# A transformer block on one core: one burst of value products a head, four side slots, and halves and sums made on other engines

## What is computed

```
mod = (silu(c) @ wmod).reshape(4, 6, 1, 512);  sa, ca, ga, sb, cb, gb = mod[:, 0..5]
ga, gb = sign * maximum(abs, 0.25)
h = layernorm(x) * (1 + ca) + sa
q = (h @ q_w.T + q_b) as 16 heads of 32;  k = h @ k_w.T + k_b;  v = h @ v_w.T + v_b
scores = q @ k.T / sqrt(32), future keys masked
x = x + ga * (softmax(scores) @ v, heads joined, @ o_w.T + o_b)
h = layernorm(x) * (1 + cb) + sb
h = fwht(h * SU_ug) / 64
h = silu(h @ W_gate.T * s_gate) * (h @ W_up.T * s_up)
x = x + gb * (fwht(h * SU_dp) / 64 @ W_down.T * s_dp)
```

## Time and profile before

| | us |
|---|---|
| median of three runs | 1978.73 |
| lowest and highest | 1975.44, 1981.24 |
| the profiled execution, its own time | 1982.4 |
| its span | 1980.6 |
| attention, heads 0 to 63, within it | about 57 to 904 |
| TensorE busy | 1902.7 |
| VectorE busy | 1392.6 |
| ScalarE busy | 833.0 |
| GpSimd busy | 462.1 |

### The profile page before, as it was taken

The page is one execution under the profiler, slowest core; times in us unless marked ns, Lnnn a source line. Parts: engine busy times, 40 slices in busy tenths (PEclk is TensorE's granted clock), DMA queues, the critical chain, the costliest instruction groups (busy, mean ns, idle before and its releaser), DMA issues.

```text
span 1980.6 us, 39650 instructions
## 1 busy us (share of the span) xinstructions
PE 1902.7 (96%) x15040; PEld 1582.5 (80%) x15040; DVE 1392.6 (70%) x3247; ACT 833.0 (42%) x1551; POOL 462.1 (23%) x525
## 2 busy tenths in 40 slices
PE   6999999999999999999999999999999999999998
PEld 3677777777777667667888789999999999999997
DVE  6788787777668666684467797777676777767755
ACT  3366455555555554473222442333333323333221
POOL 2244455445444444362010010010000100101000
PEclk8899999999999999999999999999999999999999
DMA  7432243333332455635347989778788797887884
GB/s 228 131 97 67 77 122 102 94 82 96 107 109 60 130 167 172 221 123 177 138 138 281 359 312 347 286 288 333 287 314 323 294 345 287 291 329 290 330 306 165
DMA packets 118709, 416.19 MB, mean 210 GB/s; under 512 B 26349, under 2 KB 39917, under 8 KB 104313
## 3 DMA queue, kind: packets, MB, share of 16 engines
q1 hardware_dynamic: 106856, 363.27, 53.7%
q10 hardware_dynamic: 11664, 50.40, 6.7%
HBM read 318.16 MB, written 61.10 MB: 191 GB/s over the span
## 4 chain that ended last, share of the span: by engine, by line
PE 46%; DVE 5%; ACT 2%; DMA 1%; issue 1%; SPq 0%; POOL 0%; DVEq 0%; ACTq 0%
PE banks L1810 22%; PE banks L1900 15%; PE banks L1680 8%; PE banks L1776 1%; DVE ln_stats L1254 1%; PE banks L1770 1%; DMA upgate_items_dram<-items_ring 1%; DVE x_normed L1266 0%; DVE y L1379 0%; DMA upgate_raw<-in_w_ug 0%; ACT silu_gate L911 0%; ACT y_split L896 0%; ACT L911 0%; ACT L917 0%; DVE out_sb L1451 0%
## 5 line engine op out<-in xcount | busy, mean ns | idle before, releaser
L1900 PE MATMUL banks<-d_ring,y_split 128*128 128x512 f32 x1536 | 377.6, 393 | 1.9 <-DVE y_split L1399 1.9
L1007 ACT ACTIVATE probs<-banks 128x512 f32<-128x512 f32 x576 | 314.8, 600 | 149.6 <-PE banks L1946 145.7
L1900 PEld LDWEIGHTS banks<-d_ring,y_split 128*128 128x128 f32 x1536 | 281.9, 188 | 56.6 <-DVE y_split L1399 2.1
L1810 PE MATMUL banks<-h_t_split,items_ring 128*128 128x256 f32 x2280 | 321.2, 284 | 1.9 <-DVE both L1356 1.9
L1810 PEld LDWEIGHTS banks<-h_t_split,items_ring 128*128 128x128 f32 x2280 | 299.0, 191 | 13.7 <-ACT h_t L822 4.0
L1734 PE MATMUL banks<-k_stack,q_stacks 96*128 96x512 f32 (+3 forms) x768 | 255.5, 376 | 26.7 <-DVE max_all L1166 12.4
L1946 PE MATMUL banks<-q_stacks,k_stack 98*128 98x512 f32 (+3 forms) x768 | 254.2, 373 | 4.5 <-DMA q_stacks<-neg_max_rows 3.9
L1810 PE MATMUL banks<-input_sums,items_ring 128*128 128x256 f32 x1710 | 236.2, 283 | 0.0
L1108 POOL TENSOR_TENSOR probs<-probs 128x1024 f32<-128x1024 f32 x64 | 153.4, 2396 | 334.0 <-ACT probs L1007 334.0
L1978 PE MATMUL banks<-probs,values 128*32 128x128 f32 (+1 forms) x3328 | 222.8, 322 | 3.1 <-POOL probs L1128 3.1
L1810 PEld LDWEIGHTS banks<-input_sums,items_ring 128*128 128x128 f32 x1710 | 218.9, 192 | 0.0
(11 more groups left out here) (180 smaller groups left out, 2715.1 us busy)
## 6 DMA issues: line engine op xcount, KB each, us to landing
items_ring<-upgate_items_dram SPq DMA_DIRECT2D x94, 1792.0 KB, 7.3
d_ring<-down_split_dram SPq DMA_DIRECT2D x128, 512.0 KB, 8.1
q_stacks<-q_split SPq DMA_DIRECT2D x192, 128.0 KB, 2.9
upgate_raw<-in_w_ug SPq DMA_DIRECT2D x32, 512.0 KB, 4.8
upgate_items_dram<-items_ring ACTq DMA_DIRECT2D x8, 1792.0 KB, 7.5
upgate_items_dram<-items_made ACTq DMA_DIRECT2D x8, 1792.0 KB, 6.7
x<-in_x SPq DMA_DIRECT2D x32, 256.0 KB, 3.0
o_group<-o_and_sums SPq DMA_DIRECT2D x256, 32.0 KB
```

Of the source, the lines that this page charges most:

```text
L1007: nc.scalar.activation(pr[:, probs_slot(H, u), :], score_bank[:, at % SLOTS_SCORE, :], ACT.Exp, scale=SCALE).then_inc(exped, 1)
L1810: last = nc.tensor.matmul(item_bank(g, item), weights[:, a, item, k * P:(k + 1) * P], by_key(item_input(blk, item, m))[:, k, :], start=(k ...
L1900: last = nc.tensor.matmul(acc[:, t, :], ys[s][:, a, t * P:(t + 1) * P], dr[g % D_RING][:, m, :], start=(f == 0 and a + m == 0), stop=(f == ...
```

## The change

Four things are changed together.

- **The burst.** `weigh` runs both parts of head H - 1 one behind the other after unit 5 of head H. The table WEIGHED is laid out anew: part 0 has 14 instructions where it had 21, part 1 has 23 where it had 24. Part 1 still waits for GpSimd's sums and masks. GpSimd adds the probabilities of unit 7 too (`sum_last`, a third add of 512 columns behind the last masks of the head), so the products of unit 7's blocks with ones fall away. The transposition of the maxima moves from unit 2, where it stood ahead of the maxima product, to unit 5, behind it. ScalarE still copies it behind the exponential of unit 2, in the order of its own program.
- **The banks.** All heads share one output bank; the part 0 of a head waits until the head before has been evacuated. The bank that comes free is a fourth side slot.
- **High halves.** `modulate` and `keys_values` on ScalarE read the slot twice and write the rounded high half themselves, ahead of the unrounded copy; the two casts on VectorE are gone.
- **Folds.** The w_down tiles at unit 4 move to unit 5. Their two sets of loads share one set of semaphores.

The core of the diff:

```diff
 PART_ENDS, PARTS_OF_HEAD = (4, 8), 2
+WEIGH_UNIT, SCORES_AHEAD = 5, 3
 WEIGHED = [
-    [(0, 0, (0, 4)), (1, 0, (1, 5)), (2, 0, (2, 6)), (3, 0, (3, 7)), (0, "sum", ((0, 3), (6, 7))), (1, "sum", ((0, 2), (6, 6))),
+    [(0, 0, (0, 4)), (1, 0, (1, 5)), (2, 0, (2, 6)), (3, 0, (3, 7)), (0, "sum", ((0, 3), (6, 7))), (1, "sum", ((6, 6),)),
...
-    if 0 < H < heads - 1:
-        units[TOP_UNIT].append(("top", H + 1))
     if 0 < H < heads - AHEAD:
         for i in range(NS):
             units[i].append(("max", H + AHEAD, i))
+    if 0 < H < heads - 1:
+        units[WEIGH_UNIT].append(("top", H + 1))
...
-    SLOTS_SCORE, SLOTS_SIDE = 3, 3
-    score_bank, side, obank = banks[:, 0:3, :], banks[:, 3:6, :], banks[:, 6:8, :]
+    SLOTS_SCORE, SLOTS_SIDE = SCORES_AHEAD, 4
+    score_bank, side, obank = banks[:, 0:3, :], banks[:, 3:7, :], banks[:, 7, :]
...
-                nc.scalar.activation(kv[:, i % 2 * HALF:(i % 2 + 1) * HALF], side[:, r, :], ACT.Identity,
-                                     bias=mod[:, 0, k, b:b + 1], scale=mod[:, 1, k, b:b + 1]).then_inc(side_free[r], 1)
+                for out in (ht[:, 0, k, h * HALF:(h + 1) * HALF], kv[:, i % 2 * HALF:(i % 2 + 1) * HALF]):
+                    last = nc.scalar.activation(out, side[:, r, :], ACT.Identity, bias=mod[:, 0, k, b:b + 1], scale=mod[:, 1, k, b:b + 1])
+                last.then_inc(side_free[r], 1)
...
                     side_step(ends[u])
-                    if u == PART_ENDS[0] and H:
+                    if u == WEIGH_UNIT and H:
                         evacuate(H - 1)
-                    side_step(units[u])
+                    side_step([key for key in units[u] if key[0] != "top" or H == 0])
+                    if u == WEIGH_UNIT - SCORES_AHEAD and H:
+                        side_step([key for key in units[WEIGH_UNIT] if key[0] == "top"])
...
+            def sum_last(H):
+                pool.wait_ge(summed, 3 * H + 2)
+                pool.wait_ge(masked, H * len(TRIANGLES) + list(TRIANGLES).index(SUM_AFTER) + 1)
+                nc.gpsimd.tensor_tensor(pr[:, PR_SLOTS - 2, :], pr[:, PR_SLOTS - 2, :], pr[:, probs_slot(H, SUM_AFTER), :], ALU.add).then_inc(summed, 1)
...
-                chain.link(nc.vector.tensor_copy(ht[:, 0, k, at], kv[:, i % 2 * HALF:(i % 2 + 1) * HALF]))
...
-                chain.link(nc.vector.tensor_copy(kst[0:96, b % 2, at], kv[0:96, at]))
...
-                    if H >= 2:
-                        pe.wait_ge(o_copied, H - 1)
+                    if H:
+                        pe.wait_ge(o_copied, H)
...
-                    if u == PART_ENDS[0] and H:
-                        weigh(H - 1, 1)
-                    if u == (PART_ENDS[1] if H else FIRST_WEIGHED):
-                        weigh(H, 0)
-            weigh(ALL - 1, 1)
+                    if u == WEIGH_UNIT and H:
+                        for part in range(PARTS_OF_HEAD):
+                            weigh(H - 1, part)
+            for part in range(PARTS_OF_HEAD):
+                weigh(ALL - 1, part)
```

More of the change, by code:

```diff
@@ L52 @@
 WEIGHED = [
[L53 to L60 removed]
+    [(0, 0, (0, 4)), (1, 0, (1, 5)), (2, 0, (2, 6)), (3, 0, (3, 7)), (0, "sum", ((0, 3), (6, 7))), (1, "sum", ((6, 6),)),
+     (2, 1, (2, 6)), (3, 1, (3, 7)), (1, 1, (1, 5)), (0, 1, (4,)), (2, 2, (2, 6)), (3, 2, (3, 7)), (0, 2, (4,)), (1, 2, (5,))],
+    [(0, 3, (4,)), (1, 3, (5,)), (2, 6, (6,)), (3, 3, (3, 7)), (0, 4, (4,)), (1, "sum", ((0, 2),)), (2, 3, (6,)),
+     (0, "sum", ((1, 3), (5, 7))), (1, 4, (5,)), (2, 4, (6,)), (3, 6, (7,)), (1, 5, (5,)), (2, 5, (6,)), (3, 4, (7,)),
+     (0, "sum", ((3, 3), (7, 7))), (1, "sum", ((1, 2), (5, 6))), (2, "sum", ((0, 1), (5, 5))), (3, 5, (7,)), (3, 7, (7,)),
+     (0, "sum", ((2, 3), ("all", 7))), (1, "sum", ((2, 2), ("all", 6))), (2, "sum", ((1, 1), ("all", 5))),
+     (3, "sum", ((0, 0), ("all", 4)))],
 ]
@@ L92 @@
 PART_ROWS = 32
-PART_BANKS = (6, 7)
+PART_BANKS = (2, 7)
 BESIDE_MAXIMA = {("max", 0, 2 * k + 1): k for k in range(KT)}
@@ L100 @@
 PROJECTION_STEPS = (1, 5)
-FOLDS = [("across", left, u) for left, us in ((18, (4, 8)), (17, (4, 8)), (16, (4, 8)), (15, (2, 4, 6, 8)), (14, (4, 8)), (13, (4, 8)), (12, (4, 8))) for u in us]
-FOLDS += [("along", left, u) for left, us in ((10, (4, 8)), (9, (4, 8)), (8, (4, 8)), (7, (2, 4, 6, 8)), (6, (4, 8)), (5, (4, 8)), (4, (4, 8))) for u in us]
+FOLDS = [("across", left, u) for left, us in ((18, (5, 8)), (17, (5, 8)), (16, (5, 8)), (15, (2, 4, 6, 8)), (14, (5, 8)), (13, (5, 8)), (12, (5, 8))) for u in us]
+FOLDS += [("along", left, u) for left, us in ((10, (5, 8)), (9, (5, 8)), (8, (5, 8)), (7, (2, 4, 6, 8)), (6, (5, 8)), (5, (5, 8)), (4, (5, 8))) for u in us]
 FOLD_RING = 4
@@ L421, in phase @@
     small_in, had_ready = sem("ffn_small_in"), sem("had_ready")
-    across_in, raw_in, again_in = sem("across_in"), [sem(f"raw_in{n}") for n in range(FOLD_RING)], [sem(f"again_in{n}") for n in range(FOLD_RING)]
+    across_in, fold_in = sem("across_in"), [sem(f"fold_in{n}") for n in range(FOLD_RING)]
     fold_hi, fold_out = sem("fold_hi"), [sem(f"fold_out{n}") for n in range(2)]
@@ L754, in keys_values @@
                 r = side_filled(act, key)
-                nc.scalar.activation(kv[:, h * HALF:(h + 1) * HALF], side[:, r, :], ACT.Identity, bias=kvb[:]).then_inc(side_free[r], 1)
+                at = slice(h * HALF, (h + 1) * HALF)
+                nc.scalar.activation(kst[0:96, key[1] % 2, at], side[0:96, r, :], ACT.Identity, bias=kvb[0:96])
+                nc.scalar.activation(kv[:, at], side[:, r, :], ACT.Identity, bias=kvb[:]).then_inc(side_free[r], 1)
             def values(key):
@@ L981, in evacuate @@
                     act.wait_ge(gathered[H % 2], 80 * (H // 2))
-                nc.scalar.activation(oraw[:, H % 2, :], obank[:, H % 2, :], ACT.Copy).then_inc(o_copied, 1)
+                nc.scalar.activation(oraw[:, H % 2, :], obank, ACT.Copy).then_inc(o_copied, 1)
             def round_group(G, half):
@@ L1892, in down @@
                     if g == 0:
-                        for r in (1, 2):
+                        for r in range(1, SLOTS_SIDE):
                             side_drained(pe, r)
@@ L1976, in weigh @@
                     moving = pr_blocks(places[0], places[-1] - places[0], len(places))
-                    out = obank[row * HD:(row + 1) * HD, H % 2, first * P:(first + len(places)) * P]
+                    out = obank[row * HD:(row + 1) * HD, first * P:(first + len(places)) * P]
                     last = nc.tensor.matmul(out.rearrange("p (a n) -> p a n", n=P), weights, moving, start=row not in begun, stop=part == 1 and last_of[row] == i)
```

23 lines of the change are left out of this document (8 added, 15 removed).

## The result

The changed kernel takes 2053.47 us (median of four runs, 2049.16 to 2057.63), the kernel before beside it 1977.63. The ratio is 1.0377, with a 95% interval of 1.0352 to 1.0402. That is 76 us more, where 26 were forecast. The direction was right; the size lies above the range. The profiled execution took 2057.6 us, its span is 2055.9.

What follows compares the result with a forecast made beforehand. TensorE looked like the bound, VectorE close behind. Head terms summed to +23 us, the clock added 3: 1982.4 became 2008, less 3.7 for the median of runs, forecast 2005 us; range 1966 to 2032.

Steps and rivals of the forecast that it cites:

- The plain heads and those with statistics: Sixteen attention heads: seven plain go from 8.80 to 9.5 us (+5), nine with statistics from 8.84 to 10.1 (+11).
- the tie: In each head, the moved top product needs unit 2's maxima slot, so the burst waits for VectorE; period 9.2 us.
- I take two: TensorE idling lowers its clock: two half-clock stretches of 1.7 us counted, +3 us; bounds 0 and 31.
- The sign that I had named for being wrong: In the trace after: long half-clock stretches that did not stand before would show the forecast wrong.
- The third rival: Waits drop TensorE's clock in most plain and row heads, stack transfers are late: 31 us more, 2033 us; chance 10%.
- The last six heads: Heads 58 to 63: counted as fold heads, folds -5 us in all; last head's add and late ScalarE +2.
- Rows heads: Heads 9 to 11 of three batches: ScalarE's row work waits behind held exponentials; 10.81 becomes 11.85 or 12.8; +14 us.
- Heads n = 12: Three heads starting a group of four, priced within the fifteen group starts at mean +0.4 us: +1 us together.
- is hidden, narrowly: GpSimd's extra add, 1.31 us, ends at 7.0 us in head 18, before the burst's second part at 7.3.
- Output heads gain: Nine heads with output tiles give VectorE time: period 13.7 us against 14.50, together -7 us.
- The fourth slot: Waits for slots, some 0.5 us in head 18, go; with them gone TensorE alone would need about 7.9 us.
- The first rival: TensorE is the bound, VectorE ready earlier: plain, statistics and row heads gain 0.4 us each, 1962 us; chance 18%.

Runs made afterwards that it cites:

- fills: Changed kernel with unused 512-column products in TensorE's waits in heads 9 to 12 and in seven other places: 2033.87 us, ratio 1.0283.
- filled waits: Changed kernel with five unused 512-column products ahead of unit 4's maxima product in heads 9 to 12 of three batches: 2038.44 us, ratio 1.0300.

## Why the prediction was wrong, point by point

**The plain heads and those with statistics: right.** 9.5 for 9.5, 9.9 for 10.1; +13 us in all, where 16 were forecast, and it is VectorE that TensorE waits for. Only the tie is another: the larger wait is ahead of M4, for the ring of slots (0.84 us), and the smaller at T (0.19), and with T moved away from there the time did not fall. The three engines' orders and four slots were enough to find it.

**"I take two" stretches at half clock: a term of the sum that was mis-sized, 3 us for about 20.** I had the bounds, 0 and one stretch in each of 18 heads (31 us), and chose near the lower end because before has only seven stretches in 64 heads. But those seven were counted in a kernel that hardly waits. In the kernel after, the heads hold 144 us of half clock by the clock records, in the kernel before 42. With 67 us of it removed by fills, 20 us of time went. Most of the rest of the excess lies in the last six heads, where halving it brought nothing that can be measured. So the clock was worth about 20 of the 76 us, where I had 3. The sign that I had named for being wrong, long half-clock stretches that did not stand before, is there. The third rival named this mechanism. It was right for most rows heads and not for most plain ones (heads 5, 7, 15 and 31 have no half clock at all); its 1.7 us fit the slow burst (4.85 for 3.17) and not the head, which lost 1.1.

**The last six heads: not walked, and 30 us, the largest miss.** I counted them as fold heads and priced the end with one add. The "along" tiles of w_down pass through ScalarE and VectorE like rows do, and the one behind unit 5 is behind exponentials that wait for the burst. The waits of the kernel after, heads 58 to 63, in the table of waits (in total, times, longest):

```profile
DVE fold_split L1257 <- ACT fold_split L807: 18.2, 4, 5.1
ACT probs L1009 <- PE banks L1987: 14.9, 5, 4.1
PE banks L1987 <- POOL probs L1120: 4.6, 1, 4.6
```

Before, VectorE waited there 2.0 us in three times for the same tile. The last row is the last head's wait for the new add, 4.6 us, where before it waited 2.7 for the masks and I had 1.3 more. I had seen the chain through ScalarE in the rows heads and didn't ask which others have it. One burst on top of the slots costs 23.6 us here, the third add 13.5, the place of the tiles perhaps 6; they don't add up. Undoing the burst's place in the full change gives back only 8 of the 30 us (91 for 99), undoing the third add 7.6. So no one part makes this loss, and how the 30 us divide stays open.

**Rows heads: nearly right but for the clock.** I had 11.85, or 12.8 if VectorE meets GpSimd's add, and took +1.5 a head, between the two: +14 for nine. At full clock (filled waits) heads 10 and 11 take 12.7 us and the nine together 112.8, +15.4; what lies above that, up to +21.9, went with the half clock. VectorE does meet GpSimd, in the negation of head 10 of the kernel after and not in the second subtraction: it took 1.24 us where it takes 0.17 alone.

```profile
180.89 1.28 POOL L1114 TENSOR_TENSOR probs<-probs 128x512 f32<-128x512 f32 x1
...
180.96 1.24 DVE L1190 SCALAR_TENSOR_TENSOR neg_max<-max_all,neg_max 128x8 fp32r<-128x8 f32 x1
```

**Heads n = 12: a mis-sized term, 1 us for 12.7.** They join both: rows whose low halves the next queries wait for, and a group start. I gave group starts a mean of 0.4; these three lost 4.2 each, and 3.0 each with the clock held up by the fills.

**GpSimd's third add "is hidden, narrowly": wrong.** It is hidden from the burst in every head but the last, but not from VectorE. It cost 21 us in the full change, and 11 or 35 with two bursts, depending on the rest.

**Output heads gain: half right.** Those with n = 6 and 7 gained 0.5 us each (57.9 to 55.9 us in four); n = 5, behind a group start, lost 2.4 in heads 21 and 37, each of which has a stretch of half clock that it did not have before.

**The fourth slot: never priced as a gain by itself.** The prediction names waits for slots of some 0.5 us a head in passing and treats the slot as a detail of the burst. Alone it is worth 41 us. Of the change, then, in this order of adding: four slots -41, one burst +99, and the third add, the other place of the tiles and the high halves together +18; in another order the parts get other prices, as the third add has shown. The first rival, that TensorE is the bound, did not come true. With the slots alone head 31 fits it (8.46 us, TensorE busy throughout); with three adds GpSimd's loop sets the pace, with one burst VectorE's chain.

## What to carry to other kernels

Price each part of a bundled change alone, the favourable ones too: the best kernel here was a quarter of the change. When two bursts become one, ask what every other engine may do meanwhile (here: as much as the slots hold), and list all work that stands behind the held instructions, not only that of the commonest stage. Where a change brings waits to TensorE, a count of half-clock stretches from the old trace is no estimate; price what stands behind the waits at the lower level as well, and treat that as an upper estimate (here a burst lost 1.7 us and its head 1.1).

## What the runs showed of the hardware

- Useless products in TensorE's waits made the kernel faster by 15 us: in head 10 the granted clock stayed at 1.00 and a burst of 74 matmuls took 3.19 us instead of 4.85. In the last six heads the same measure brought nothing, and in heads 17 and 33 it only moved the half clock to the head behind.
- GpSimd and VectorE slow each other. A negation of 128 x 8 elements, begun 0.07 us behind a GpSimd add of 1.28, took 1.24 us instead of 0.17; a GpSimd add of 128 x 512 took 2.24 instead of 1.27, three masks 4.00 instead of 1.0.
- A view that shows TensorE as busy for all of a head doesn't say that it can't go faster: 8.80 us busy became 8.46 by a slot more, with the same products.
